# Rotary partner rows by a shuffle instead of a second product, in a two-layer transformer kernel on one core

## The reference

```python
def _rope(t):                       # t: batch, tokens, 16 heads, 8 features
    half = Dh // 2
    inv_freq = 1.0 / ROPE_BASE ** (jnp.arange(half) / half)
    ang = jnp.arange(L)[:, None] * inv_freq[None, :]
    cos, sin = jnp.cos(ang)[None, :, None, :], jnp.sin(ang)[None, :, None, :]
    t1, t2 = t[..., :half], t[..., half:]
    return jnp.concatenate([t1 * cos - t2 * sin, t2 * cos + t1 * sin], axis=-1)

q, k, v = jnp.split(xn @ qkv_w.T, 3, axis=-1)     # second layer, self-attention
sa = _attn(_rope(q), _rope(k), v) @ sa_out_w.T    # the same follows with keys of the context
```

## Time and profile before

| | before |
|---|---|
| median of 3 runs | 383.92 us (382.63 to 384.54) |
| profiled execution, own time | 385.06 us |
| its span, first to last instruction | 383.3 us |
| granted TensorE clock, mean over the span | 0.964 of full |
| busy PE, DVE, ACT, POOL | 363.0, 301.7, 254.5, 100.6 us |

### The profile page before, as it was taken

One profiled execution on the slowest core, in us unless ns is written; L12 is line 12 of the kernel. 1 busy time (PEld: TensorE's weight loads), 2 busy tenths in 40 slices (PEclk: granted clock), 3 DMA queues, 4 the chain that ended last, 5 costly groups with the idle time before them and its releaser, 6 DMA issues.

```text
span 383.3 us, 12514 instructions
## 1 busy us (share of the span) xinstructions
PE 363.0 (95%) x5090; PEld 260.6 (68%) x5090; DVE 301.7 (79%) x809; ACT 254.5 (66%) x513; POOL 100.6 (26%) x120
## 2 busy tenths in 40 slices
PE   7699999999999999999999999999999899999996
PEld 3485687677776776657654567666677577886776
DVE  5985989999999998947999839997799747875302
ACT  2525965578676987889453797378766945688551
POOL 6920310142020201125351234343413401031130
PEclk9966999999999999999999999999999957999999
DMA  8673244005221360014050140403140404000003
GB/s 208 259 240 93 78 140 167 9 27 186 84 88 43 127 219 5 3 32 169 2 193 6 29 168 7 169 5 106 65 168 4 168 8 159 8 3 3 2 0 111
DMA packets 19757, 34.13 MB, mean 89 GB/s; under 512 B 2740, under 2 KB 7988, under 8 KB 19700
## 3 DMA queue, kind: packets, MB, share of 16 engines
q1 hardware_dynamic: 19268, 33.24, 25.2%
q10 hardware_dynamic: 432, 0.09, 0.2%
HBM read 6.51 MB, written 1.05 MB: 20 GB/s over the span
## 4 chain that ended last, share of the span: by engine, by line
PE 55%; DVE 4%; ACT 3%; DMA 3%; SPq 3%; issue 2%; ACTq 0%; DVEq 0%
PE ps_ao L1058 11%; PE ps_misc L999 8%; PE ps_misc L1028 6%; PE ps_misc L1109 6%; PE ps_misc L1087 6%; PE ps_misc L1025 6%; PE ps_misc L935 3%; PE ps_misc L1094 3%; DVE maxima L690 3%; PE ps_misc L1068 2%; PE ps_misc L1007 2%; ACT PT L882 2%; DMA Ks<-Kl 2%; DMA Ks<-Kh 1%; SPq L537 1%
## 5 line engine op out<-in xcount | busy, mean ns | idle before, releaser
L690 DVE TENSOR_REDUCE maxima<-ps_misc 128x4 f32<-128x512 f32 (+1 forms) x256 | 153.5, 664 | 17.6 <-PE ps_misc L1025 17.1
L882 ACT ACTIVATE PT<-ps_misc 128x512 f32<-128x512 f32 (+1 forms) x256 | 131.7, 606 | 24.0 <-PE ps_misc L1028 22.7
L1058 PE MATMUL ps_ao<-PT,V 120*18 120x128 f32 (+1 forms) x2048 | 70.5, 282 | 0.5 <-ACT PT L882 0.5
L1025 PEld LDWEIGHTS ps_misc<-Ks,Qd 32*128 32x128 f32 x1024 | 41.9, 197 | 30.8 <-issue 11.3
L1025 PE MATMUL ps_misc<-Ks,Qd 32*128 32x128 f32 (+1 forms) x1024 | 53.4, 298 | 8.5 <-DMA Ks<-Kl 3.3
L1058 PEld LDWEIGHTS ps_ao<-PT,V 120*18 120x18 f32 (+1 forms) x2048 | 52.6, 101 | 7.4 <-issue 2.3
L1028 PEld LDWEIGHTS ps_misc<-Qd,Ks 32*128 32x128 f32 (+1 forms) x1024 | 38.0, 186 | 21.5 <-issue 13.7
L752 POOL TENSOR_SCALAR vareps<-mv 128x4 f32<-128x4 f32 (+1 forms) x28 | 6.4, 228 | 170.9 <-DVE mv L595 170.6
L1028 PE MATMUL ps_misc<-Qd,Ks 32*128 32x128 f32 (+1 forms) x1024 | 48.7, 287 | 1.5 <-DVE maxima L690 0.8
L866 ACT ACTIVATE xnT<-ps_misc,vec 128x128 f32<-128x128 f32 x80 | 30.1, 462 | 15.6 <-PE ps_misc L935 15.5
L999 PE MATMUL ps_misc<-xnT,Wr 128*128 128x512 f32 x72 | 37.5, 641 | 1.8 <-ACT xnT L866 1.6
(11 more groups left out here) (83 smaller groups left out, 449.7 us busy)
## 6 DMA issues: line engine op xcount, KB each, us to landing
Qd<-Qh SPq DMA_DIRECT2D x32, 256.0 KB
Ks<-Kh SPq DMA_DIRECT2D x16, 256.0 KB, 2.9
Qd<-Ql SPq DMA_DIRECT2D x16, 256.0 KB
Ks<-Kh SPq DMA_DIRECT2D x16, 240.0 KB, 2.4
Ks<-Kl SPq DMA_DIRECT2D x8, 256.0 KB, 3.0
Ks<-Kl SPq DMA_DIRECT2D x8, 240.0 KB, 2.5
x<-x_in SPq DMA_DIRECT2D x4, 256.0 KB, 6.0
W<-weights SPq DMA_DIRECT2D x2, 512.0 KB, 5.0
```

The source lines that it names most:

```text
L690: dve.tensor_reduce(maxima[:, h, st.b % HB, c, :], bank(use + c)[:, 0:NG * ns].rearrange("p (n k) -> p n k", n=NG), AX_X, ALU.max, negate= ...
L882: act.activation(PT[0:ns, k % PSLOTS, c, :, :].rearrange("p n t -> p (n t)"), bank(use + c)[0:ns, :], ACT.Exp, scale=SCALE).then_inc(S["pr ...
L1025: ins = pe.matmul(bank(st.use + c)[:, n * ns:(n + 1) * ns], queries, keys, start=True, stop=True)
L1058: last = pe.matmul(ps_ao[32 * c:32 * c + PAIR, block * P:(block + 1) * P], heads[:, at:at + PAIR], PT[0:ns, k % PSLOTS, c, n, :], start=no ...
```

## The change

The swapped weights go: `q2s`, `k2s`, `q3s`, `k3s` leave the weight tensor (512 of its columns) and `Wr`, and `q.f` and `k.f` of a rotary feed become one product in one bank. VectorE multiplies it by the cosines as before, and in place of the second multiplication shuffles the same bank into `ropeB`, partition i from partition i+16 modulo 32. GpSimd multiplies `ropeB` by the sines in place, and then adds.

```diff
-                    for i, dst, table in ((0, ropeA, "cos"), (1, ropeB, "sin")):
-                        dve.wait_ge(S["misc_filled"], use + i + 1)
-                        dve.tensor_tensor(dst[:, int(not k), 0:n].rearrange("p (b t) -> p b t", b=CB),
-                                          bank(use + i)[:, 0:n].rearrange("p (b t) -> p b t", b=CB),
-                                          const(table)[:, None, 0:ns].to_broadcast([P, CB, ns]),
-                                          ALU.mult).then_inc(S["rope_read"], 1)
+                    dve.wait_ge(S["misc_filled"], use + 1)
+                    dve.tensor_tensor(ropeA[:, int(not k), 0:n].rearrange("p (b t) -> p b t", b=CB),
+                                      bank(use)[:, 0:n].rearrange("p (b t) -> p b t", b=CB),
+                                      const("cos")[:, None, 0:ns].to_broadcast([P, CB, ns]),
+                                      ALU.mult).then_inc(S["rope_read"], 1)
+                    dve.stream_shuffle(ropeB[:, int(not k), 0:n], bank(use)[:, 0:n],
+                                       TURNED_ROWS).then_inc(S["rope_read"], 1)
...
-                        total = ropeA[:, int(not k), 0:n]
-                        pool.tensor_tensor(total, total, ropeB[:, int(not k), 0:n],
-                                           ALU.add).then_inc(S["rope_sums"], 1)
+                        total, turned = ropeA[:, int(not k), 0:n], ropeB[:, int(not k), 0:n]
+                        blocks = turned.rearrange("p (b t) -> p b t", b=CB)
+                        pool.tensor_tensor(blocks, blocks,
+                                           const("sin")[:, None, 0:n // CB].to_broadcast([P, CB, n // CB]),
+                                           ALU.mult).then_inc(S["rope_turned"], 1)
+                        rope_sums_made += 1
+                        pool.wait_ge(S["rope_turned"], rope_sums_made)
+                        pool.tensor_tensor(total, total, turned, ALU.add).then_inc(S["rope_sums"], 1)
...
-                        for i, form in enumerate(forms):
-                            fill(st.use + i)
-                            pe.matmul(bank(st.use + i)[:, 0:n], w_rows(f"{st.kind}{st.a}{form}"), src[:, 0:n],
-                                      start=True, stop=True).then_inc(S["misc_filled"], 1)
+                        fill(st.use)
+                        pe.matmul(bank(st.use)[:, 0:n], w_rows(f"{st.kind}{st.a}"), src[:, 0:n], start=True,
+                                  stop=True).then_inc(S["misc_filled"], 1)
...
                     elif st.kind in ("max", "score"):
+                        taken = st.name in BESIDE
+                        if taken:
+                            for c in range(HG):
+                                fill(st.use + c)
+                            keep_going(st)
```

```diff
-        h.m3.2 h.m3.0 max.9.2 h2.m3 xT.10 mT.9.0 score.8.0 yT.m3 q.10 k.10 score.8.1 v.10 max.9.3 xT.11 value.8.0
+        h.m3.0 h.m3.1 max.9.2 h2.m3 xT.10 score.8.0 yT.m3 q.10 score.8.1 k.10 value.8.0 score.8.2 max.9.3 v.10
```

More of the change, by code:

```diff
@@ L31 @@
 HB = CB // 2
+TURNED_ROWS = [(i + TROWS // 2) % TROWS for i in range(TROWS)]
 FF = 4
@@ L42 @@
 BESIDE = {
[3 rows of a table removed]
+    "xT.0": 2, "max.0.0": 2, "xT.3": 2, "mT.1.0": 1, "norm.1.1": 1, "xT.5": 1, "norm.5.1": 1, "norm.7.0": 1,
+    "out.6": 1, "norm.7.1": 1, "xT.m3": 1, "mT.8.1": 1, "norm.8.0": 1, "norm.9.1": 1, "out.9": 4, "mT.12.0": 1,
+    "norm.12.1": 1, "aT.12": 1, "mT.15.0": 1,
 }
@@ new lines @@
+        mT.3.0 xT.4 yT.1 value.2.1 q.4 score.2.3 k.5 value.2.2 max.3.3 value.2.3 xT.5 score.3.0 norm.2.1 norm.2.0
+        q.5 mT.3.1 score.3.1 max.4.0 value.3.0 aT.2 max.4.1 value.3.1 score.3.2 max.4.2 mT.4.0 v.5 o.2 score.3.3
+        value.3.2 max.4.3 score.4.0 value.3.3 yT.2 norm.3.0 score.4.1 mT.4.1 norm.3.1 value.4.0 max.5.0 score.4.2
+        aT.3 max.5.1 value.4.1 score.4.3 o.3 max.5.2 mT.5.0 xT.6 value.4.2 max.5.3 value.4.3 cT.2 q.6 norm.4.1 yT.3
+        score.5.0 mT.5.1 norm.4.0 k.6 v.6 cT.3 aT.4 score.5.1 k.7 out.4 score.5.2 value.5.0 xT.7 max.6.0 value.5.1
@@ new lines @@
+        score.5.3 q.7 norm.5.0 v.7 max.6.1 value.5.2 value.5.3 xT.m0 norm.5.1 max.6.2 mT.6.0 h.m0.3 aT.5 h.m0.1
+        max.6.3 h.m0.0 h.m0.2 out.5 score.6.0 max.7.0 h2.m0 mT.6.1 score.6.1 value.6.0 xT.m1 yT.m0 max.7.1
+        score.6.2 value.6.1 h.m1.3 max.7.2 mT.7.0 h.m1.0 h.m1.2 h.m1.1 max.7.3 value.6.2 score.6.3 score.7.0 xT.8
+        h2.m1 value.6.3 k.8 mT.7.1 score.7.1 q.8 norm.6.0 norm.6.1 yT.m1 score.7.2 value.7.0 aT.6 value.7.1 out.6
+        score.7.3 norm.7.0 v.8 value.7.2 value.7.3 xT.9 max.8.0 norm.7.1 xT.m2 k.9 q.9 aT.7 h.m2.1 max.8.1 h.m2.3
@@ new lines @@
+        score.10.1 max.11.2 value.10.0 score.10.2 value.10.1 mT.11.0 max.11.3 xT.13 value.10.2 score.10.3 norm.10.0
+        q.13 k.14 score.11.0 value.10.3 score.11.1 mT.11.1 norm.10.1 value.11.0 max.12.0 max.12.1 aT.10 score.11.2
+        value.11.1 max.12.2 mT.12.0 out.10 score.11.3 norm.11.0 value.11.2 max.12.3 value.11.3 v.12 k.15 score.12.0
+        v.13 mT.12.1 norm.11.1 max.13.0 xT.14 value.12.0 max.13.1 aT.11 q.14 score.12.1 v.14 mT.13.0 out.11
+        score.12.2 max.13.2 value.12.1 score.12.3 value.12.2 max.13.3 score.13.0 xT.15 value.12.3 norm.12.0 mT.13.1
@@ new lines @@
+        q.15 score.13.1 max.14.0 value.13.0 score.13.2 norm.12.1 max.14.1 value.13.1 score.13.3 norm.13.0 max.14.2
+        mT.14.0 value.13.2 max.14.3 value.13.3 score.14.0 norm.13.1 v.15 mT.14.1 score.14.1 max.15.0 value.14.0
+        aT.12 max.15.1 score.14.2 out.12 value.14.1 max.15.2 mT.15.0 aT.13 score.14.3 value.14.2 max.15.3
+        score.15.0 out.13 value.14.3 mT.15.1 score.15.1 norm.14.0 xT.m4 norm.14.1 value.15.0 value.15.1 score.15.2
+        h.m4.3 h.m4.2 aT.14 score.15.3 norm.15.0 out.14 xT.m5 value.15.2 value.15.3 h.m4.1 norm.15.1 h.m5.3 h.m5.1
@@ L224, in __init__ @@
         self.engine = engine
-USES = {"k": 2, "q": 2, "max": HG, "score": HG, "value": 0, "warm": 0}
+USES = {"max": HG, "score": HG, "value": 0, "warm": 0}
 def uses_of(st):
-    if st.kind in ("k", "q"):
-        return 2 if ATTN[st.a]["rope"] else 1
     return USES.get(st.kind, 1)
@@ L1021, in _ @@
                                 queries = Qd[rows, st.f % KSLOTS, n, st.b * P:(st.b + 1) * P]
-                                if n == 0:
+                                if n == 0 and not taken:
                                     fill(st.use + c)
```

187 lines of the change are left out of this document (84 added, 103 removed), and 3 rows, old and new, of the table BESIDE.

## The result

The changed kernel takes 420.93 us as a median (417.11 to 428.20 in four runs), the kernel before 383.27 in the runs beside it: a ratio of 1.095, 95% interval 1.085 to 1.105. The forecast was 374.5 with a range to 382.5, so the sign was wrong. Runs of one kernel scatter here by one to three per cent, and the mean granted clock scatters with them; where a profiled execution was the longest of its kernel, that is said.

A forecast was written before the change was run, and what follows sets the result against it. TensorE's order was taken to bound the rotary part. The terms -10.9 + 0 + 0 + 1.0 + 0.5 = -9.4 brought the profiled 385.06 to 375.7 us; less 1.14, a median of 374.5 us, eight-in-ten range 367.5 to 382.5.

The forecast's parts named there:

- The new lists as such I count at 0.: Over the whole kernel, the new order of steps was taken to cost or gain nothing: 0 us.
- Identity products: 0.: On TensorE, 25 units for 30 save 1.1 to 2.1 us but only fill waits, so 0 was taken.
- Sixteen products removed: -10.9.: In the rotary part, 12.9 us leave TensorE's chain, of which VectorE lets 10.9 us be gained.
- The cap that I took from the first layer's 89%: VectorE's busy share without rotary steps, 89.3%, taken as sustainable, lets the rotary part shrink from 157 to 146.1 us.
- VectorE as full as now: Rival, rotary part: VectorE's share does not rise and TensorE's freed time becomes waits; no change, 383.9 us, chance 0.10.
- GpSimd's delay: +1.0; contention: +0.5.: Rotary feeds: later sums on GpSimd expose 0.8 to 5.1 us, 1.0 taken; slower VectorE norms 0 to 9.5, 0.5 taken.
- Shuffle for multiplication: 0, at most +0.7.: On VectorE, sixteen shuffles in place of multiplications change its work by -3.1 to +0.7 us; 0 taken.
- The rival of the clock: Stretches at half clock: one more 380.4 us, chance 0.14; two more 386.3, 0.05; one fewer 368.6, 0.17.
- my price: A stretch of 13.44 us at the low clock would have been 7.5 at full, so costs up to 5.9 us.
- the rotary chain binds: Rival, rotary feeds: moves wait for GpSimd in all eight, 20.5 us in, at most 12.9 out; 391.5 us, chance 0.07.
- the signs of failure that I had listed: TensorE's key waits beyond 1 or 2 us, a third half-clock stretch, shuffles well over 0.72 us, or an unshortened rotary part.

The follow-up runs named there:

- e11: The changed kernel without the sixteen multiplications by the sines on GpSimd: 420.98 us.
- e1: The changed kernel with the order lists, identity products and banks (less those for second products) of the kernel before: 396.01 us, ratio 1.034.
- e14: The kernel before with other bank numbers only, six PSUM banks instead of seven from feed 4's first maximum to feed 5's last: 391.22 us, ratio 1.018.
- e4: The kernel before with the changed kernel's table of identity products (25 units) in place of its own: 395.46 us, ratio 1.037.
- e3: The changed kernel with the larger number of the two identity-product tables at each step, 48 units: 421.82 us.
- e12: Old lists, single rotary products, multiplications by the sines left out, and identity products added ahead of the first maxima of feeds 10, 11, 13 and 14: 388.00 us.
- e2: The kernel before with the new lists and identity products, and a bank added for each of the sixteen second products: 440.35 us, ratio 1.154.
- e8: The changed kernel with the old lists up to the transposes of feed 10 and the new ones behind: 396.78 us, ratio 1.043.

## Why the prediction was wrong, point by point

**"The new lists as such I count at 0."** This is the step that failed. Up to the first maximum of feed 8, where but for that feed's own products only lists and identity products differ, the changed kernel loses 24.9 us (`e11`, the same kernel up to there, 20.9) and `e1` with the old ones 0.5. What the runs showed in place of the 0 is a loss of some 25 of 38 us by the lists with their table (420.93 against 396.01 in `e1`). Their waits for banks are seen in the trace, and `e14` shows that such waits cost time; that they make the whole of the lists' loss is not shown. I compared numbers (25 units for 30) and a few rows of the order; I did not ask whether the banks of a maximum are free when its turn comes.

**"Identity products: 0."** Wrong. The total hardly changed, but the places did, and they count: 13 us in the old lists (`e4`). I had also misread the tables: from `xT.8` on they do not both have 12 units, but 12 before and 15 after, and ahead of `xT.8` 18 before and 10 after. So the part without rotary work lost eight units. In the new lists the table is not the cause alone (`e3`).

**"Sixteen products removed: -10.9."** Wrong in mechanism. The rows were read rightly: the products were 8% of the chain. But a chain says what was last in one execution, not how far behind the next work is. In the old lists taking them out costs 4 to 10 us, and at best (`e12`) the chain goes over to VectorE and ScalarE. The cap that I took from the first layer's 89% does not hold for the rotary part, which stayed at 77 to 83%. The rival "VectorE as full as now" had this mechanism, with a chance of 0.10. Whether lists made for single products use the time is open: in the new lists the old rotary part is 19 us slower (`e2`), but 9.0 of them are waits for the banks that I chose; and single products in the new lists from feed 10 on (`e8`) are no faster than in the old ones.

**"GpSimd's delay: +1.0; contention: +0.5."** In the new lists both together are about 0 (`e11`). In the old lists the sum is 4 to 10 us. With the second products kept the sizes were the wrong way round: the norms took 6.0 us more, in the upper part of my 0 to 9.5, and the keys' waits 0.7. The Trainium skill, page "GPSIMD Engine Reference", section "1. Specifications", names SBUF interfaces that GpSimd shares with VectorE; the 363 against 425 ns agree. With the second products gone the keys' waits grew by 2.7 us, so the delay was put too small as well.

**"Shuffle for multiplication: 0, at most +0.7."** The shuffles of after are slower than the multiplications by 0.7 us in all; its VectorE groups:

```profile
L620 DVE STREAM_SHUFFLE ropeB<-ps_misc 128x512 f32<-128x512 f32 x12 | 8.8, 731 | 0.0
L620 DVE STREAM_SHUFFLE ropeB<-ps_misc 128x480 f32<-128x480 f32 x4 | 2.8, 694 | 0.0
```

The estimate of 0.71 us from the Trainium skill, page "VectorE: DVE Perf Modes", section "The perf-mode tier table", was nearer than the 678 ns behind my 0.

**The rival of the clock.** Right in kind, far too small in number: I gave one or two stretches more 0.19, and 47 us more came. I had tied a stretch to a single long wait. After, some of the eleven follow such a wait again (the 1.6 us for exponentials and the 1.5 for keys above stand ahead of two), but others follow shorter ones: ahead of 59.7 us TensorE was busy 5.66 of 6.80 us, and a value step then takes 1.91 us as in the earlier trace rows:

```profile
52.90:59.70 6.80, 5.66 (x106) 4.42 (x104) 4.77 (x13) 4.03 (x10) 0.00 (x0) 1.00 0.02 5
```

```profile
58.87 0.32 PE L1035 MATMUL ps_misc<-Ks,Qd 32*128 32x128 f32 x1 [0.74 <-ACT PT L887]
59.36 0.80 PE L1035 MATMUL ps_misc<-Ks,Qd 32*128 32x128 f32 x14 [0.17 <-ACT PT L887]
60.09 1.91 PE L1068 MATMUL ps_ao<-PT,V 128*18 128x128 f32 x32
```

How much of the loss is the clock can be estimated in two ways. By my price, 5.9 us for a stretch of 13.44, the 47 us more at half clock are 47 x 0.44 = 21 us. By runs of after at different clocks, 417.11 us at 0.925 and 421.94 at 0.911, 0.01 is 3.45 us, and the 0.053 between the two profiled kernels 18 us. So 18 to 21 of 36.9 us. The rest is near the 18.9 us by which TensorE's idle time grew (span less busy time, 20.3 to 39.2), 11.7 of them in further waits for banks as named above. No run separates the two in the changed kernel, where falls of the clock come behind such waits, as at 59.7 us.

**The rival "the rotary chain binds"** is what `e1` shows at feeds 10 and 11, and what the changed kernel avoids. Of the signs of failure that I had listed, two came: the third stretch at half clock, and a part no shorter in which VectorE waits for maxima. Over the whole span its idle time ahead of the maxima doubled, before and after:

```profile
L690 DVE TENSOR_REDUCE maxima<-ps_misc 128x4 f32<-128x512 f32 (+1 forms) x256 | 153.5, 664 | 17.6 <-PE ps_misc L1025 17.1
L690 DVE TENSOR_REDUCE maxima<-ps_misc 128x4 f32<-128x512 f32 (+1 forms) x256 | 153.4, 664 | 34.4 <-PE ps_misc L1035 34.0
```

## What to carry to other kernels

A new order is a change of its own, and where an order was written out by hand it may be the largest: follow the buffers (here seven PSUM banks) through the new order before counting it at nothing, above all in parts that the edit doesn't touch. Work taken off the engine that the chain of waits names is a gain only if the next engine has room at that place; here it left holes, and the clock fell in them. An edit in the old order, and the new order without the edit, separate what two profiles mix.
